# Fused cross-attention on one core: all transpositions of x by VectorE, two operand tiles, other PSUM banks, last pairs reordered

## The reference

```
# layer 0, per sample; rgb = x.T, geo = ctx.T (1024 x 128)
xca(q, k, v): attn = softmax(einsum('bhni,bhnj->bhij', q, k) * scale); out = einsum('bhnd,bhde->bhne', v, attn)
res_p2r = xca(heads(rgb, wq_rgb), heads(geo, wk_point), heads(geo, wv_point)) @ proj_p2r.T
res_r2p = xca(heads(geo, wq_point), heads(rgb, wk_rgb), heads(rgb, wv_rgb)) @ proj_r2p.T
x = transpose(rgb + res_p2r) + transpose(geo + res_r2p)
# layer 1, y = ctx
q = conv1x1(Wq, bq, y); k = conv1x1(Wk, bk, y); v = conv1x1(Wv, bv, x)
attn = softmax(einsum('bhdl,bhel->bhde', q, k) / sqrt(E))
o = conv1x1(Wo, bo, einsum('bhde,bhel->bhdl', attn, v)) + x
out = (o - mean(o)) * rsqrt(var(o) + eps) * gn_w + gn_b      # mean and var over the whole sample
```

## Time and profile before

| | us |
|---|---|
| median of 3 runs | 336.96 (336.56 to 337.16) |
| the profiled execution | 336.94 |
| its span, first to last instruction | 335.2 |
| TensorE busy | 313.4 (94%) |
| VectorE busy | 263.8 (79%) |
| ScalarE busy | 231.2 (69%) |
| GpSimd busy | 190.4 (57%) |
| mean granted TensorE clock | 0.982 of full |

### The profile page before, as it was taken

One profiled execution on the slowest core, in us unless ns is written; L12 is line 12 of the kernel. 1 busy time (PEld: TensorE's weight loads), 2 busy tenths in 40 slices (PEclk: granted clock), 3 DMA queues, 4 the chain that ended last, 5 costly groups with the idle time before them and its releaser, 6 DMA issues.

```text
span 335.2 us, 12612 instructions
## 1 busy us (share of the span) xinstructions
PE 313.4 (94%) x4808; PEld 273.0 (81%) x4808; DVE 263.8 (79%) x716; ACT 231.2 (69%) x382; POOL 190.4 (57%) x277
## 2 busy tenths in 40 slices
PE   6999999999978999999999999999999999994980
PEld 3887898989866898988888898989898888972760
DVE  1595888988985788888898889888888999653574
ACT  3653757878785787878787797878787878954332
POOL 0874482757676275767667575757676675754010
PEclk9999999999999999999999999999999999997897
DMA  7999989498989949797998989797979670300215
GB/s 224 389 258 300 261 230 245 162 276 225 284 230 299 232 123 285 226 297 214 305 244 251 283 210 319 195 298 217 287 221 299 174 250 1 125 0 22 105 47 204
DMA packets 39061, 73.88 MB, mean 220 GB/s; under 512 B 4608, under 2 KB 26368, under 8 KB 39040
## 3 DMA queue, kind: packets, MB, share of 16 engines
q1 hardware_dynamic: 35008, 58.92, 64.6%
q10 hardware_dynamic: 4032, 14.68, 12.2%
HBM read 56.81 MB, written 16.78 MB: 220 GB/s over the span
## 4 chain that ended last, share of the span: by engine, by line
PE 88%; issue 3%; DVE 2%; POOL 2%; DMA 2%; ACT 2%; SPq 0%; POOLq 0%; ACTq 0%
PE oacc L429 10%; PE oacc L436 9%; PE oacc L430 9%; PE mid L526 5%; PE mid L454 4%; PE gacc L391 4%; PE mid L503 4%; PE stat L393 4%; PE tpx L348 4%; PE gacc L392 3%; PE gacc L393 3%; PE stat L392 3%; PE stat L391 3%; PE mid L512 2%; PE gacc L409 2%
## 5 line engine op out<-in xcount | busy, mean ns | idle before, releaser
L1129 POOL TENSOR_TENSOR xy_lo<-raw,xy_hi 128x256 fp32r<-128x256 f32 x256 | 179.9, 740 | 116.5 <-ACT xy_hi L696 116.5
L696 ACT ACTIVATE xy_hi<-raw 128x1024 fp32r<-128x1024 f32 x64 | 66.9, 1048 | 0.0
L856 DVE STREAM_TRANSPOSE t<-y_blocks 128x512 f32<-128x512 f32 x56 | 62.9, 1162 | 0.0
L429 PE MATMUL oacc<-xy_hi,pq_hi 128*128 128x512 f32 x124 | 55.6, 448 | 5.0 <-ACT res L703 4.8
L885 DVE BATCH_NORM_STATS2 hstat<-res 128x6 f32<-128x512 f32 x60 | 40.1, 688 | 22.8 <-ACT res L703 22.7
L703 ACT ACTIVATE res<-oacc 128x512 f32<-128x512 f32 x60 | 35.6, 594 | 30.7 <-PE oacc L436 30.4
L430 PE MATMUL oacc<-xy_lo,pq_hi 128*128 128x512 f32 x124 | 50.0, 403 | 1.5 <-issue 1.5
L394 PE MATMUL gacc<-t 128*32 128x225 f32 x224 | 45.4, 354 | 0.0
L393 PE MATMUL gacc<-t 128*32 128x225 f32 x224 | 45.4, 354 | 0.0
L394 PE MATMUL stat<-t 128*32 128x225 f32 x224 | 44.9, 353 | 0.0
L393 PE MATMUL stat<-t 128*32 128x225 f32 x224 | 44.9, 353 | 0.0
(11 more groups left out here) (146 smaller groups left out, 916.8 us busy)
## 6 DMA issues: line engine op xcount, KB each, us to landing
raw<-in_x SPq DMA_DIRECT2D x31, 512.0 KB, 5.7
raw<-in_ctx SPq DMA_DIRECT2D x31, 512.0 KB, 7.0
y_blocks<-in_ctx SPq DMA_DIRECT2D x112, 128.0 KB, 7.0
out<-res ACTq DMA_DIRECT2D x28, 512.0 KB, 3.4
x_blocks<-in_x SPq DMA_DIRECT2D x56, 128.0 KB, 6.7
out<-res SPq DMA_DIRECT2D x4, 512.0 KB, 2.8
wt<-in_weights SPq DMA_DIRECT2D x1, 896.0 KB, 7.0
raw<-in_x SPq DMA_DIRECT2D x2, 256.0 KB, 3.7
```

Of the source, the lines that this page charges most:

```text
L429: pe.matmul(bank[:, :], whi, xy_hi[slot][:, s, cols], start=(s == 0), stop=False)
L696: act.activation(xy_hi[slot][:, s, :], raw[slot][:, s, :], ACT.Copy).then_inc(split_hi, 1)
L856: dve.transpose(dst, blocks[:, HC * i:HC * (i + 1)]).then_inc(yt_ready, 1)
L1129: piece = pool.tensor_tensor(xy_lo[slot][:, s, cols], raw[slot][:, s, cols], xy_hi[slot][:, s, cols].bitcast(f32), ALU.subtract)
```

## The change

- **x by VectorE.** From step 2 on TensorE turns no x; VectorE turns x of both samples from blocks, loaded a second time. Sample 3 is also turned by VectorE (before: by TensorE). ScalarE's copies of those transpositions go. Per pair there are eight transpositions of 128x512 on VectorE, where six were.
- **Two t tiles** in place of four; a transposition for sample n waits for the Gram products of sample n - 2.
- **Banks.** u12, u3, the scores and probabilities stand in the two tpx banks. u12_products no longer waits for the shift of the pair before, u3_products no longer for pq_lo; z_operands waits for both.
- **Value bias by TensorE**: three VectorE instructions per pair go, one two-pass product becomes two (L506).
- **Statistics**: partition_moments and variance do the same with other instructions.
- **Order.** TensorE: pq, u12 and u3 follow each other at the head of a step, and the four products with pq_hi of both halves stand before those with pq_lo. VectorE: u3_out stands before pq_low.
- **Head.** Two block loads for sample 3 come in, and x and y of that sample come later. The mask is made before the weights are scaled.
- **Last pairs.** Step 16 makes pq of both last pairs and interleaves output products with z, m and pq; ScalarE's norm_scale stands last in that step. The last step writes into four banks.

```diff
-TB = 4
+TB = 2
...
+        tail = [tpx[i].rearrange("p m r -> p (m r)") for i in range(2)]
+        u12_bank, u3_bank = tail[0], tail[1][:, 0:2 * C]
+        o_next = [oacc, [gacc, oacc[0]]]
+        o_last = [tail, [oacc[1], gacc]]
...
             sp.dma_start(w_rot[H64:C, :, :], weights[0:H64, k:k + 2, :]).then_inc(weights_in, 16)
-            for n in range(2, 4):
-                load_x(0, n)
-                load_y(0, n)
+            load_x(0, 2)
+            load_y(0, 2)
+            sp.dma_start(vec_rot[0:H64, :], vectors[H64:C, :]).then_inc(weights_in, 16)
+            sp.dma_start(vec_rot[H64:C, :], vectors[0:H64, :]).then_inc(weights_in, 16)
+            load_blocks(0, 3)
+            load_x_blocks(0, 3)
             load_blocks(1, 0)
+            load_x_blocks(1, 0)
+            load_x(0, 3)
+            load_y(0, 3)
             load_blocks(1, 1)
-            load_x_blocks(1, 0)
+            load_x_blocks(1, 1)
...
                 sp.wait_ge(yt_ready, 2 * n + 2)
                 load_blocks(h + 1, 2 * u + b)
-                if b == 1:
-                    sp.wait_ge(xt_ready[1], n + 1)
-                    load_x_blocks(h + 1, u)
+                sp.wait_ge(xt_ready[b], n - b + 2)
+                load_x_blocks(h + 1, 2 * u + b)
...
             def z_operands(p):
                 pe.wait_ge(attn_ready, p + 1)
+                if not (isinstance(p, int) and p < 1):
+                    pe.wait_ge(c_ready, p)
+                    pe.wait_ge(pqlo_ready, p)
...
-                pe.wait_ge(abv_ready, p + 1)
-                pe.matmul(mid0[:, 2 * C:2 * C + 2], w("oT"), abv[:, :], start=True, stop=True)\
-                    .then_inc(wo_abv_done, 1)
+                for a in range(2):
+                    mm = pe.matmul(mid0[:, 2 * C + a:2 * C + a + 1], z[:, a, 2, :], (col("bv"), col("bv", vec_rot))[a],
+                                   start=True, stop=True)
+                mm.then_inc(wo_bv_done, 1)
...
                 elif front:
-                    x_transpose(h, u, 0)
                     pq_products(p - 2)
-                    x_transpose(h, u, 1)
                     u12_products(p - 1)
-                    out_half(h - 1, u, 0, 0)
                     u3_products(p - 1)
+                    out_half(h - 1, u, 0, 0, parts=(0,))
+                    out_half(h - 1, u, 0, 1, parts=(0,))
+                    out_half(h - 1, u, 0, 0, parts=(1,))
+                    out_half(h - 1, u, 0, 1, parts=(1,))
                     if post:
                         group_moments(p - 3)
-                    out_half(h - 1, u, 0, 1)
                     scores(p - 1)
...
                 elif middle:
+                    n = 4 * (h - 1) + 2 * u
+                    u12_products(p - 1)
+                    u3_products(p - 1)
                     pq_products(p - 2)
-                    u12_products(p - 1)
-                    group_moments(p - 3)
-                    u3_products(p - 1)
-                    out_half(h - 1, u, 0, 0)
                     scores(p - 1)
-                    out_half(h - 1, u, 0, 1)
-                    out_half(h - 1, u, 1, 0)
-                    out_half(h - 1, u, 1, 1)
+                    out_half(h - 1, u, 0, 0, parts=(0,))
+                    out_half(h - 1, u, 0, 1, parts=(0,))
+                    out_half(h - 1, u, 0, 0, parts=(1,))
+                    out_half(h - 1, u, 0, 1, parts=(1,))
                     z_operands(p - 1)
                     keep_warm(1)
                     z_products(p - 1)
-                    keep_warm(4)
+                    out_half(h - 1, u, 1, 0, banks=o_next, bank_free=0)
+                    group_moments(p - 3)
                     m_products(p - 1, True)
-                    keep_warm(2)
+                    out_half(h - 1, u, 1, 1, parts=(0,), banks=o_next, bank_free=2 * n + 3)
+                    pq_products(p - 1)
+                    out_half(h - 1, u, 1, 1, parts=(1,), banks=o_next)
                 else:
-                    pq_products(p - 2)
-                    keep_warm(2)
...
                 elif middle:
-                    pq_high(p - 2, u)
                     u12_out(p - 1)
                     keys_times_sums(p - 1)
+                    pq_high(p - 2, u)
                     split_high(h - 1, 1, 1, 0, True)
+                    exponent(p - 1)
                     split_high(h - 1, 1, 1, 1, True)
+                    out_to_sbuf(h - 1, u, 0, 0)
+                    out_to_sbuf(h - 1, u, 0, 1)
+                    z_out_last(p - 1)
+                    out_to_sbuf(h - 1, u, 1, 0, o_next)
+                    pq_high(p - 1, 1 - u)
+                    out_to_sbuf(h - 1, u, 1, 1, o_next)
                     norm_scale(p - 3)
-                    out_to_sbuf(h - 1, u, 0, 0)
                     normalise(*before(h, u), 0)
...
                 elif front:
                     if post:
                         half_stats(*before(h, u), 1, 1)
                         half_moments(p - 3)
                         partition_moments(p - 3, 1 - u)
+                    u3_out(p - 1)
                     pq_low(p - 2, u)
+                    x_transpose(h, u, 0, 1)
                     y_transpose(h, u, 1, 0)
-                    y_transpose(h, u, 1, 1)
-                    u3_out(p - 1)
+                    x_transpose(h, u, 1, 0)
                     if post:
                         variance(p - 3, 1 - u)
-                    x_transpose(h, u, 0)
                     shift_scores(p - 1)
-                    x_transpose(h, u, 1)
+                    y_transpose(h, u, 1, 1)
+                    x_transpose(h, u, 1, 1)
                     softmax_out(p - 1)
                     half_stats(h - 1, u, 0, 0)
                     half_stats(h - 1, u, 0, 1)
                     if ahead:
                         y_transpose(h + u, 1 - u, 0, 0)
+                        x_transpose(h + u, 1 - u, 0, 0)
+                    gram_mirror(p)
+                    if ahead:
                         y_transpose(h + u, 1 - u, 0, 1)
-                    gram_mirror(p)
                     half_stats(h - 1, u, 1, 0)
                     n12_out(p - 1)
                     n3_out(p - 1)
                     c_out(p - 1, 1 - u)
```

More of the change, by code:

```diff
@@ L408, in gram_full_width, with out_half @@
                 for c in range(begin, end):
-                    mm = pe.matmul(gacc_b[b], t[n][:, c, 0:C], t[n][:, c, :], start=(c == 0), stop=(c == CH - 1))
+                    mm = pe.matmul(gacc_b[b], t[b][:, c, 0:C], t[b][:, c, :], start=(c == 0), stop=(c == CH - 1))
                 if end == CH:
                     mm.then_inc(gram_done, 1)
-            def out_half(h, u, b, half, last=False, parts=range(2)):
-                bank = o_last[b][half] if last else oacc[half]
+            def out_half(h, u, b, half, parts=range(2), banks=(oacc, oacc), bank_free=None):
+                bank = banks[b][half]
                 slot = 2 * u + b
@@ L820, in _, with prepare_mask, prepare_weights @@
             dve.wait_ge(attn_zero, 2 * QUADS)
-            def prepare():
+            def prepare_mask():
+                s1 = float(C) ** -0.5
                 dve.wait_ge(consts_in, 16)
-                dve.wait_ge(weights_in, 80)
+                dve.wait_ge(small_in, 32)
+                dve.tensor_scalar(nbq[:, :], col("bq"), s1 * N, None, ALU.mult).then_inc(mask_ready, 1)
+                dve.tensor_copy(mask6[:, 0:4, :], other_head.unsqueeze(1).broadcast_to([C, 4, W32]))
+                dve.wait_ge(mask_ready, 1)
+                for a in range(2):
+                    last = dve.scalar_tensor_tensor(out=mask6[:, 4 + a, :], in0=bk32, scalar=nbq[:, :],
+                                                    in1=other_head, op0=ALU.mult, op1=ALU.add)
+                last.then_inc(mask_ready, 1)
+            def prepare_weights():
+                dve.wait_ge(weights_in, 16 * 5)
                 s0, s1 = float(C // H) ** -0.5, float(C) ** -0.5
@@ L904, in partition_moments @@
                 dve.wait_ge(c_ready, p + 1)
[L905 removed]
                 dve.tensor_tensor(mom[:, 0, bs], pstat[:, bs, 0], cshift[u][:, bs], ALU.add).then_inc(mean_ready, 1)
                 dve.wait_ge(mean_ready, count)
[L908 to L910 removed]
+                for b in range(bs.start, bs.stop):
+                    mean = mom[:, 0, b:b + 1]
+                    last = dve.scalar_tensor_tensor(out=mom[:, 1, b:b + 1], in0=mean, scalar=mean,
+                                                    in1=pstat[:, b, 1:2], op0=ALU.mult, op1=ALU.add)
+                last.then_inc(mom_ready, 1)
             def variance(p, u, bs=BOTH):
```

284 lines of the change are left out of this document (120 added, 164 removed).

## The result

The changed kernel takes **346.62 us** (median of 4 runs, 344.4 to 348.5) against 336.76 us of the kernel before in the same session: a ratio of **1.029**, 95% interval 1.023 to 1.036. I had said 332.9 us. The profiled execution took 346.65 us, its span is 344.9. The first part of its page answers to the earlier trace rows; its columns are the same.

The account below looks back on a forecast made before the run. TensorE bounds the old loop, VectorE 1.7 us below it and the new bound. Span 335.2 + 8.9 (loop) + 0.1 (head) - 13.0 (closing) = 331.2 us, plus 1.74 outside the span: 332.9 us, range 327.5 to 339.5.

Parts of the forecast that it names:

- The loop step: Settled loop: VectorE's 17.0 us plus a 2.4 us round through TensorE, taken as 19.3 us against 18.38.
- Rival A: Loop: loads become the bound since a step moves ten pieces, not nine; 21.3 us a step, 349 us; chance 0.08.
- Rivals B and C: Loop, n3_out to u3_out: round longer, 19.9 us a step, 340 us, chance 0.12; or round hidden, 326 us, 0.08.
- The two waits of step 5: TensorE waits of 1.77 and 1.54 us; half of 3.8 us was to vanish in slack, -1.9 us.
- +8.9 us: Whole loop: 11.0 us for 12 longer steps, step 2 about 0.2 shorter, -1.9 in step 5.
- My rival for the loads: Loop: ten load pieces a step, 5.24 MB, become the bound; 349 us, chance 0.08.
- The head: Before the loop: TensorE's gain and VectorE's loss nearly cancel at z, +0.1 us, between -0.5 and +2.
- The closing: Last steps: norm_scale wait gone, full clock, gaps filled; -13.0 us, between -10.5 and -14.5.
- -11.6: Step 16: norm_scale's wait -4.8, full clock -2.6, filled time before step 17 -3.5, shorter waits at its head -0.7.
- The last step: End of the closing: without its pq and with ScalarE free, -1.4 us.
- my 12 steps: Loop: 12 steps between the pq copies at 53.42 and 277.85, each 19.3 for 18.38 us, 11.0 us more.

Follow-up runs that it names:

- the third session's pair: Kernel after with loads of samples 4 to 7 held back, 345.98 us; the same plus the rotated vector's own semaphore and VectorE's second x transposition ahead of u3_out, 336.09 us.
- the closing alone: Kernel before with only the new order of the last steps, scores of the last pair in the transposition banks: 326.73 us, ratio 0.965.
- the kernel with held loads: Kernel after with SyncE holding back loads of samples 4 to 7 to about 10 us before first use, all data loaded: 345.98 us, ratio 1.019.

## Why the prediction was wrong, step by step

The predicted span was 331.2 us, the measured one 344.9; three terms make up the 13.7 us: the loop with steps 2 to 5 (10.3), the head (2.2) and the closing (1.2).

- **The loop step: right, and its mechanism too.** 19.3 us, with VectorE's only idle time before u3_out (0.85 to 0.93 us, I had 0.7 to 0.8) and TensorE late to pq. Rival A did not happen as I put it: at 273 GB/s no transposition of the loop waits for its blocks. Rivals B and C fell with the 19.3.
- **The two waits of step 5: this step failed.** From the first copy to that of step 15 I had +8.9 us; it is (299.36 - 37.10) - (277.85 - 34.82) = +19.2. I saw the waits "ended by nothing that the trace shows", let half of them vanish in TensorE's slack (-1.9) and asked no further. They were late instruction blocks. What decides them is not slack but, while code runs for the first time, how full the queues are and how fast TensorE runs through 256 instructions. The waits grew from 3.3 to 11.7 us, two half-clock stretches came behind them, and steps 2 to 5 were 10.4 us longer than my sum had them (88.6 against 18.4 + 3 x 19.3 + 1.9 = 78.2). My rival for the loads priced bytes per loop step, the one place where they cost nothing.
- **The head: +0.1 predicted, +2.3 measured.** The part that failed is the list of what the head waits for. The two new loads of the rotated vector count on the semaphore of the weights, so the weights' scaling waited until 18.20 us; with another semaphore the copy stood at 34.92. By the traces above that is 1.1 to 2.2 us, but only 0.1 in the third session's pair, so what the semaphore costs is open. I had kept +2 as a bound, but for late blocks, which is not what happened.
- **The closing: -13.0 predicted, -11.8 measured.** Step 16 itself went as argued: 22.55 us became 329.35 - 318.81 = 10.54, -12.0 against -11.6, with full clock and no gap of TensorE over 1 us before the last statistics. The last step gave about -1.0 (I had -1.4). Mis-sized was step 15: it has the loop's form and takes 19.45 us where it took 18.27, and my 12 steps left these +1.2 us out.

The sign turned on the second point: with its 10.3 us taken out the span is 334.6 us against 335.2 before. Without the early x blocks, which a right result needs, the same instructions are 1.5% faster than the kernel before, at a span of 332.9 us: no border wait was left there, where my sum had kept 1.9 us.

What stays open: why in the kernel before the 16 KB packets for borders 961 and 1473 began 1.1 us after the border before, and those for 1217 and 1985 2.8 and 2.3 us. I put it down to the gaps in its queues (share 0.86 from 40 to 60 us), but a packet for border 2497 began 4.9 us late at a share of 0.87; which loads a packet stands behind can't be seen in these traces. Whether other engines' instruction packets (8 KB each, on q14) ever come late was not tried.

## What to carry to other kernels

A wait that nothing in the trace ends is not noise: count all of the engine's instructions up to it, and if such waits lie 256 apart, each 1.2 to 1.6 us behind a 16 KB packet of the instruction queue, the price of more loads in the first pass is late code, and every change of the load traffic or of the instruction count there moves it. When two engines are within 2 us of each other in a step, as here, work moved from one to the other may only change which one is the bound; price the round that the move closes. Judge the parts of a change one by one: here one part was worth 12 us, and the rest cost about 22.

## What the runs showed of the hardware that I had not expected

- Instructions late by up to 4.96 us in a straight run of matmuls, at the same instruction count in every trace of the same stream, with 42 waits at borders in 13 traces and all of them 1.24 to 1.62 us behind the landing of a 16 KB packet.
- Half-clock stretches of 3.4 or 6.8 us stood at waits from 1.81 us up (the closing alone), but not at all of them: the kernel after had none behind 2.02 us and 3.4 us behind 3.87 and 3.24, the kernel with held loads none behind 3.12 and 6.8 us around its wait of 3.94, and the kernel with the vector's own semaphore 6.8 us around its wait of 4.96.
- Extra loads of 0.5 MB a step cost nothing in the settled loop (18.38 to 18.43 us in the kernel before with them, at a DMA share of 1.06). With them the first pass had 10.0 us of border waits, without them 3.3 and 5.4 us in two traces.
